# A third buffer for the experts' gate and up weights, a loop body of six experts, and variance tiles of 99 columns

## The reference

```python
def layernorm(x):                       # 34 half-norms in the kernel, two halves of 296 tokens
    m = mean(x); v = mean((x - m) ** 2)
    return (x - m) / sqrt(v + eps)

# experts: each of the 16 takes up to 74 tokens (CAP), I = 1024
h = gelu(x_e @ Wg[e].T) * (x_e @ Wu[e].T)      # gate and up: 256 -> 1024 each
out[tokens of e] += score * (h @ Wd[e].T)      # down: 1024 -> 256, scattered back
```

## Time and profile before

| | us |
|---|---|
| median of three runs | 789.15 |
| the profiled execution, its time | 787.6 |
| its span, first to last instruction | 785.8 |
| PE busy | 757.9 (96%) |
| tokens, block 0 and routing (0 to 131) | 131 |
| experts (131 to 267.7) | 136.7 |
| one encoder layer (380.5 to 451.2) | 70.7 |

### The profile page before, as it was taken

How to read it: one execution, slowest core, us unless ns; L and a number is a source line. 1 busy time by engine, 2 the same in 40 slices (tenths; PEclk the granted TensorE clock), 3 DMA queues, 4 the chain that set the end, 5 groups by cost and what they waited for, 6 DMA issues and landing times.

```text
span 785.8 us, 19872 instructions
## 1 busy us (share of the span) xinstructions
PE 757.9 (96%) x7780; PEld 701.5 (89%) x7780; DVE 555.1 (71%) x1209; ACT 426.7 (54%) x816; POOL 247.6 (32%) x299
## 2 busy tenths in 40 slices
PE   9999999899899899999999999999999999999988
PEld 8898779898898898999899999989899999989758
DVE  6787593344453377787879787787879787776796
ACT  3387422222122265757776786877678677735421
POOL 0002130211111003643462465256346614633020
PEclk9999999899999999999999999999999999999999
DMA  6001745989999220101200310111031003200001
GB/s 199 1 11 45 316 144 185 387 316 378 375 381 380 84 111 2 41 15 54 75 20 13 107 40 13 42 65 40 13 107 40 0 13 107 110 2 1 1 1 32
DMA packets 16726, 83.82 MB, mean 107 GB/s; under 512 B 2848, under 2 KB 8496, under 8 KB 10672
## 3 DMA queue, kind: packets, MB, share of 16 engines
q1 hardware_dynamic: 16688, 83.30, 29.0%
HBM read 80.50 MB, written 2.79 MB: 106 GB/s over the span
## 4 chain that ended last, share of the span: by engine, by line
PE 38%; issue 25%; POOL 19%; DVE 8%; DMA 8%; ACT 3%; POOLq 0%; SPq 0%; DVEq 0%; ACTq 0%
DMA arena<-ew_in 8%; POOL W_L L2058 7%; PE bank L1179 6%; POOL HF_L L2116 4%; POOL arena L2034 3%; PE bank L741 3%; PE bank L1212 3%; POOL WQKV_L L2058 3%; PE bank L765 2%; PE bank L891 2%; PE bank L1068 2%; PE bank L924 2%; PE bank L807 1%; POOL SQ L2077 1%; PE bank L1160 1%
## 5 line engine op out<-in xcount | busy, mean ns | idle before, releaser
L2034 POOL TENSOR_TENSOR arena<-arena,srec 111x456 f32<-111x456 f32 x56 | 52.3, 961 | 122.7 <-DVE srec L2211 122.7
L1179 PE MATMUL bank<-XGS,arena 128*64 128x74 f32 x2048 | 74.5, 231 | 9.6 <-DMA arena<-ew_in 7.1
L1179 PEld LDWEIGHTS bank<-XGS,arena 128*64 128x64 f32 x2048 | 70.5, 139 | 13.7 <-issue 13.4
L2058 POOL TENSOR_TENSOR W_L<-LW,W_H 128x256 fp32r<-128x256 f32 x96 | 68.5, 749 | 36.9 <-DVE XHL L2622 33.5
L2116 POOL TENSOR_TENSOR HF_L<-arena,HF_H 128x296 fp32r<-128x296 f32 x48 | 43.9, 937 | 76.8 <-ACT HF_H L1949 76.8
L807 PE MATMUL bank<-XHL,W_H 128*128 128x296 f32 x288 | 65.1, 307 | 0.0
L1949 ACT ACTIVATE arena<-bank,vec 128x296 f32<-128x296 f32 x96 | 48.8, 509 | 20.4 <-PE bank L807 15.5
L1376 PE MATMUL bank<-HF_L,W_H 128*128 128x296 f32 x192 | 57.4, 299 | 0.0
L1376 PE MATMUL bank<-HF_H,W_H 128*128 128x296 f32 x192 | 57.4, 299 | 0.0
L1376 PE MATMUL bank<-HF_H,W_L 128*128 128x296 f32 x192 | 57.3, 299 | 0.0
L891 PE MATMUL bank<-arena 114*128 114x111 f32 x448 | 55.1, 276 | 0.7 <-issue 0.6
(11 more groups left out here) (282 smaller groups left out, 2052.3 us busy)
## 6 DMA issues: line engine op xcount, KB each, us to landing
arena<-ew_in SPq DMA_DIRECT2D x16, 2048.0 KB, 10.3
arena<-ew_in SPq DMA_DIRECT2D x16, 1024.0 KB, 7.1
LW<-lw_in SPq DMA_DIRECT2D x12, 1024.0 KB, 4.9
LW<-lw_in SPq DMA_DIRECT2D x6, 768.0 KB, 4.4
fp_weights<-arena SPq DMA_DIRECT2D x1, 2048.0 KB, 6.4
arena<-fp_weights SPq DMA_DIRECT2D x1, 2048.0 KB, 7.3
arena<-patches_in SPq DMA_DIRECT2D x2, 864.0 KB, 7.8
LW<-lw_in SPq DMA_DIRECT2D x6, 256.0 KB, 2.6
```

The costliest lines, as they stand in the source:

```text
L1179: last = mm(o[lo:lo + COL_TILE, m * CAP:(m + 1) * CAP], w[:, kc, at:at + COL_TILE], XGS[:, s, kc, :], start=(kc == 0), stop=(kc == C - 1))
L2034: nc.gpsimd.tensor_tensor(v, v, srec[0:QROWS, s:s + 2, :].unsqueeze(3).to_broadcast([QROWS, 2, C * JH, KEYS]), ALU.mult).then_inc(p_ready, 1)
L2058: last = nc.gpsimd.tensor_tensor(low[:, cols], value[:, cols], high[:, cols], ALU.subtract)
```

## The change

*A third buffer.* `GU_THIRD`, 4,096 columns, lies over `R` to `OB`; `XGS` and `EO` move behind it. Gate and up weights now rotate over three places (`GU`), down weights over two as before (`DOWN`), so that the pattern of an expert repeats every six. SP loads gate and up of expert 2 into `GU_THIRD` when the second half of the normalised tokens `U` is written (`u_ready` 2), ahead of the store of positions; and when the up product of expert k - 1 is through, `load_ahead(k)` loads gate and up of k + 2 instead of k + 1. Down of k + 1 and the routes go as before.

*The loop.* PE's body has six steps, n from 1 to 6, and runs twice; steps 13 and 14 are written out behind it. SP's body has six as well.

*The tiles.* `var_tiles` gives three starts, 0, w and nt - w, with w a third of the columns rounded up: 99 of 296, 96 of 288. The products, roots, reciprocals, subtractions and transposes work on w columns or partitions.

```diff
-        XGS = nc.alloc_sbuf_tensor_at("XGS", [P, 2, C, CAP], F32, offset=R_BASE)
+        GU_THIRD = nc.alloc_sbuf_tensor_at("GU_THIRD", [P, EGU_N], F32, offset=R_BASE)
+        XGS_BASE = R_BASE + 4 * EGU_N
+        XGS = nc.alloc_sbuf_tensor_at("XGS", [P, 2, C, CAP], F32, offset=XGS_BASE)
...
+        GU_RING = 3
+        GU = [EW[0][:, 0:EGU_N], EW[1][:, 0:EGU_N], GU_THIRD[:, :]]
...
         def var_tiles(nt):
 
-            return (0, P), (P, P), (nt - P, nt - 2 * P)
+            w = third(nt)
+            return 0, w, nt - w
+
+        def third(nt):
+
+            return -(-nt // 3)
...
+            sp.wait_ge(u_ready, 2)
+            load_gate_up(2, 2)
             sp.wait_ge(pos_cast, 1)
...
-            def load_expert(e, s, route=True):
-
-                sp.wait_ge(u_psum, e * 2 - 2)
-                load_gate_up(e, s)
-                if route:
-                    sp.wait_ge(shot_ready, e - 2)
-                    load_route(e - 1, 1 - s)
-                sp.wait_ge(d_psum, e - 1)
-                load_down(e, s)
-
-            load_expert(2, 0, False)
-            with sp.Fori(1, E // 2 - 1) as i:
-                for s in (1, 2):
-                    load_expert(i * 2 + s, s % 2)
-            load_expert(E - 1, 1)
+            def load_ahead(k, n):
+
+                sp.wait_ge(u_psum, k * 2)
+                load_gate_up(k + 2, (n + 2) % GU_RING)
+                if not isinstance(k, int) or k > 1:
+                    sp.wait_ge(shot_ready, k - 1)
+                    load_route(k, n % 2)
+                sp.wait_ge(d_psum, k)
+                load_down(k + 1, (n + 1) % 2)
+
+            load_ahead(1, 1)
+            with sp.Fori(0, 2) as i:
+                for n in range(2, 8):
+                    load_ahead(i * 6 + n, n)
...
-                        last = mm(ln_bank(seq, h)[:, at:at + VAR_W], sq[:, h, c, t0:t0 + P], ones[:, 0:VAR_W],
+                        last = mm(ln_bank(seq, h)[0:w, at:at + VAR_W], sq[:, h, c, t0:t0 + w], ones[:, 0:VAR_W],
...
-                    last = nc.tensor.transpose(ln_bank(seq, h)[:, t0:t0 + P], ln_rs[:, h, t:t + 1].to_broadcast([P, P]),
-                                               ident)
+                    last = nc.tensor.transpose(ln_bank(seq, h)[:, t0:t0 + w], ln_rs[0:w, h, t:t + 1].to_broadcast([w, P]),
+                                               ident[0:w, 0:w])
...
-            expert_step(0, 0, 1, 1, None)
-            with pe.Fori(1, E // 2) as i:
-                expert_step((i, -1, -1), 1, (i, 0, 0), 0, (i, -1, -2))
-                expert_step((i, 0, 0), 0, (i, 0, 1), 1, (i, -1, -1))
+            expert_step(0, 0)
+            with pe.Fori(0, 2) as i:
+                for n in range(1, 7):
+                    expert_step(i, n)
+            for n in range(E - 3, E - 1):
+                expert_step(0, n)
```

More of the change, by code:

```diff
@@ L300, in build @@
             PB.append(v_.bitcast(BF16)[:, 0:N])
+        GU_RING = 3
+        GU = [EW[0][:, 0:EGU_N], EW[1][:, 0:EGU_N], GU_THIRD[:, :]]
+        DOWN = [EW[s][:, EGU_N:EW_N].rearrange("p (m n) -> p m n", m=EM) for s in range(2)]
+        DOWN_FLAT = [EW[s][:, EGU_N:EW_N] for s in range(2)]
         v_, at = cut(at, C * E * CAP)
@@ L432, in build @@
         ld_qkv, ld_wo, ld_w1, ld_w2, ld_lvec = (sem(n) for n in ("ld_qkv", "ld_wo", "ld_w1", "ld_w2", "ld_lvec"))
-        ld_gu, ld_down, ld_route = ([sem(f"{n}{s}") for s in range(2)] for n in ("ld_gu", "ld_down", "ld_route"))
+        ld_gu = [sem(f"ld_gu{s}") for s in range(GU_RING)]
+        ld_down, ld_route = ([sem(f"{n}{s}") for s in range(2)] for n in ("ld_down", "ld_route"))
         route_stored, out_stored = sem("route_stored"), sem("out_stored")
@@ L761, in ln_var_of @@
                     pe.wait_ge(ln_squared, ln_count(seq, h))
-                for t, (t0, _) in enumerate(var_tiles(nt)):
+                w = third(nt)
+                for t, t0 in enumerate(var_tiles(nt)):
                     for c in range(nch):
                         at = VAR_AT + t * VAR_W
-                        last = mm(ln_bank(seq, h)[:, at:at + VAR_W], sq[:, h, c, t0:t0 + P], ones[:, 0:VAR_W],
+                        last = mm(ln_bank(seq, h)[0:w, at:at + VAR_W], sq[:, h, c, t0:t0 + w], ones[:, 0:VAR_W],
                                   start=(c == 0), stop=(c == nch - 1))
@@ L934, in patch_stats @@
                         constant_products(bank[4], 3)
-                    for t, (t0, _) in enumerate(var_tiles(NP_HALF)):
-                        last = mm(bank[5][:, at + t * VAR_W:at + (t + 1) * VAR_W], R[:, h, k, t0:t0 + P], ones_p[:, 0:VAR_W],
+                    w = third(NP_HALF)
+                    for t, t0 in enumerate(var_tiles(NP_HALF)):
+                        last = mm(bank[5][0:w, at + t * VAR_W:at + (t + 1) * VAR_W], R[:, h, k, t0:t0 + w], ones_p[:, 0:VAR_W],
                                   start=True, stop=True)
@@ L1198, in up_free, with expert_down @@
                 pe.wait_ge(hh_ready, idx(e) * 2)
-            def expert_down(e, s):
-                pe.wait_ge(ld_down[s], group(e) * 16 + 16)
+            def expert_down(e):
+                s = e[1] % 2
+                pe.wait_ge(ld_down[s], (e[0] * 3 + e[1] // 2) * 16 + 16)
                 pe.wait_ge(hh_ready, idx(e) * 2 + 2)
-                if not isinstance(e, int) or e > 0:
+                if e[1] > 0:
                     pe.wait_ge(eot_ready, idx(e))
                     pe.wait_ge(eot_split, idx(e))
-                w = EW[s][:, EGU_N:EW_N].rearrange("p (m n) -> p m n", m=EM)
+                w = DOWN[s]
                 for c in range(C):
@@ L1583, in ln_root @@
                 act.wait_ge(ln_var, ln_count(seq, h))
-                f(ln_sd[:, h, :], LNB[h][:, VAR_AT:VAR_AT + 3 * VAR_W:VAR_W], ACT.Sqrt, bias=eps1[:, :]).then_inc(ln_std, 1)
+                w = third(ln_geometry(seq)[1])
+                f(ln_sd[0:w, h, :], LNB[h][0:w, VAR_AT:VAR_AT + 3 * VAR_W:VAR_W], ACT.Sqrt, bias=eps1[0:w, :]).then_inc(ln_std, 1)
             def exponent(r, p):
@@ L1613, in enc_root @@
                 act.wait_ge(ln_var, ln_count(LN_ENC, h))
-                f(ln_sd[:, h, :], ln_bank(LN_ENC, h)[:, VAR_AT:VAR_AT + 3 * VAR_W:VAR_W], ACT.Sqrt, bias=eps_sq[:, :], scale=1.0 + EPS
+                w = third(NHALF)
+                f(ln_sd[0:w, h, :], ln_bank(LN_ENC, h)[0:w, VAR_AT:VAR_AT + 3 * VAR_W:VAR_W], ACT.Sqrt, bias=eps_sq[0:w, :], scale=1.0 + EPS
                   ).then_inc(ln_std, 1)
@@ L1640, in square_mean @@
                 act.wait_ge(patch_stats_ready, h + 1)
-                f(mean_sq[:, h, :], bank[5][:, MU_AT:MU_AT + 3 * VAR_W:VAR_W], ACT.Square).then_inc(mean_squared, 1)
+                w = third(NP_HALF)
+                f(mean_sq[0:w, h, :], bank[5][0:w, MU_AT:MU_AT + 3 * VAR_W:VAR_W], ACT.Square).then_inc(mean_squared, 1)
             def token_root(h):
@@ L1647, in token_root @@
                 act.wait_ge(ln_var, ln_count(LN_TOK, h))
+                w = third(NP_HALF)
                 for t in range(3):
-                    last = f(ln_sd[:, h, t:t + 1], LNB[h][:, VAR_AT + t * VAR_W:VAR_AT + t * VAR_W + 1], ACT.Sqrt,
-                             bias=eps_var[:, h, t:t + 1])
+                    last = f(ln_sd[0:w, h, t:t + 1], LNB[h][0:w, VAR_AT + t * VAR_W:VAR_AT + t * VAR_W + 1], ACT.Sqrt,
+                             bias=eps_var[0:w, h, t:t + 1])
                 last.then_inc(ln_std, 1)
@@ L2159, in ln_recip @@
                 dve.wait_ge(ln_std, ln_count(seq, h))
-                v.reciprocal(ln_rs[:, h, :], ln_sd[:, h, :]).then_inc(ln_rstd, 1)
+                w = third(ln_geometry(seq)[1])
+                v.reciprocal(ln_rs[0:w, h, :], ln_sd[0:w, h, :]).then_inc(ln_rstd, 1)
             def ln_scale(seq, h, out):
```

62 lines of the change are left out of this document (33 added, 29 removed).

## The result

The changed kernel takes 796.86 us (median of 4 runs, 795.32 to 799.77). The kernel before, run beside it, takes 789.47 us (788.42 to 789.85). The ratio is 1.0091, with a 95% interval from 1.0056 to 1.0127. The profiled execution took 796.79 us with a span of 794.9; before it was 787.6 with 785.8. So the span grew by 9.1 us, where the medians give 7.4: the execution profiled before is 1.9 us faster than the median.

A forecast was written before the change was run, and what follows sets the result against it. It took TensorE to bound the layers, and weight waits and late code to delay it in the expert stage. 787.6 + 18.3 (stage) - 6.5 (tiles) = 799.4 us profiled, 801 us as median; range 772 to 822.

The forecast's parts named there:

- The steps of 9 to 11 us: Sign in the expert stage: one expert's step would take 9 to 11 us instead of 8.06.
- What goes, -12.6: Expert stage: losses taken off, 7.1 us of waits for weights and 5.5 us lost in the old loop's first pass.
- step of 8.06 us: Expert stage: one expert's step from gate to gate, read as undisturbed, with no wait between.
- Code blocks, +26.9: Expert stage: 14 steps fetch 22.4 blocks of PE's code anew, at 1.2 us each.
- The jump, +4: Expert stage: the loop's one jump back finds its target gone; 4 us, between 2.1 and 8.9.
- +18.3: Expert stage in sum: 26.9 for blocks plus 4 for the jump, less 5.5 and 7.1 us.
- The clock: Sign for PE: granted clock under 1.00 in more stretches than one; half its first-pass part counted in the block price.
- The tiles, -6.5: Layer norms with 99-column tiles: 5.3 us less in the layers, 1.2 elsewhere; bounds 0 and -9.7.
- I count 5.3 in full: Layers: 24 norms at 0.22 us less each, 5.3 us, counted whole because PE is the bound there.
- The body is kept: Rival, expert stage: the six-step body stays in instruction memory, only 8 steps are new code; 785.5 us, chance 0.20.
- Fetches stay hidden: Rival, expert stage: code fetches cost PE nothing, only the removed waits count; 770 us, chance 0.17.
- middle price of 0.6 a block: Rival, expert stage: body not kept, each code block costs 0.6 us; 787.5 us, chance 0.08.

The follow-up runs named there:

- Light: The changed kernel with most gate, up and down weights of later experts cut to 256 columns, same PE instructions: 773.16 us, ratio 0.9787 to the kernel before.
- body6: The kernel before (128-column tiles, two gate-up slots) with PE's loop body of six experts alone: 804.79 us, ratio 1.0200.
- Unrolled: The changed kernel with all fourteen expert steps of PE written out, no loop and no jump back: 786.26 us, ratio 0.9960 to the kernel before.
- body2: Control: the kernel before, still two slots and a body of two, with expert helpers written as in the changed kernel: 789.06 us, ratio 0.9988.
- tiles: The kernel before with the 99-column tiles alone, two slots and the body of two kept: 782.32 us, ratio 0.9935.
- body4: The kernel before (128-column tiles, two slots) with a loop body of four experts, three passes: 791.28 us, ratio 1.0043.
- body3: The changed kernel with gate-up weights, down weights and tokens each in three slots and PE's body of three steps, four passes: 773.99 us, ratio 0.9792 to the kernel before.

## Why the prediction was right

It said 801 us and slower, for this reason: the third buffer removes the waits for weights, but the body of six doesn't stay in PE's instruction memory and loses more than that. All of it is borne out. Most of the signs that it named are there: 21 more packets (20 forecast), halts in the middle of 64 products, no wait for `ew_in`. The steps of 9 to 11 us are only half there: in the second pass they take 7.85 to 12.29 us and 15.66 at the jump. The terms are another matter; some were off and partly cancelled, so that it is in part luck how close the sum came.

**What goes, -12.6.** *Light* gives the scale: its stage without the jump's 4.35 us is 125.45, so the stage before held 138.79 - 125.45 = 13.3 us of loss. Each of these stages is that of one profiled execution, and the one before was 1.9 us below the median of its runs. The prediction had 7.1 for listed waits and 5.5 for the first pass of code, 12.6. Two of its readings were off. The step of 8.06 us that it took as undisturbed holds 0.2 us of waiting; the true one is 7.85, and the step of 7.86 from 164.23 on stood in the trace that it read. And the 7.1 us isn't the buffer's to claim under slow code: *body6* lost all but 2.2 of them with two slots. As the price of a block was charged in full beside it, the sum still comes out.

**Code blocks, +26.9.** *Unrolled* has them without a jump: 146.10 - 125.45 = 20.65 us for 14 x 1.6 = 22.4 blocks, **0.92 us a block** instead of 1.2. As that execution is 2.6 us above its median, 0.8 is the estimate for a usual one. What was mis-sized is the guess at how often a block is late and the clock falls. Only six of the blocks of *unrolled* held up PE on this line. The price depends on the run of things: one more or one less late block is up to 2 us, and *unrolled* scatters from 782.36 to 789.60 in ten runs, where the kernel before beside it goes from 787.31 to 791.85 in fifteen.

**The jump, +4.** After against *unrolled*: 153.86 - 146.10 = **7.8 us**, near the upper end of 2.1 to 8.9 that the prediction kept. By the medians it would be some 10, above that end, and the blocks would be that much cheaper. With it, 20.65 + 7.8 - 13.3 = +15.1 us, which closes by construction, where +18.3 stood: -6.3 on the blocks, +3.8 on the jump, -0.7 on what goes.

**The clock.** It was foreseen as more stretches under 1.00. Windows of the trace after; the clock is the third number from the end:

```profile
150.40:157.00 6.60, 6.60 (x75) 6.12 (x76) 3.41 (x7) 0.89 (x2) 0.00 (x0) 0.50 1.00 396
184.50:189.50 5.00, 3.06 (x70) 2.98 (x71) 0.92 (x2) 0.51 (x2) 0.62 (x1) 1.00 0.94 345
201.60:204.80 3.20, 2.57 (x42) 2.57 (x44) 1.64 (x5) 0.21 (x1) 1.07 (x1) 0.50 0.97 407
208.40:211.60 3.20, 3.20 (x57) 3.20 (x56) 0.00 (x0) 0.42 (x1) 0.00 (x0) 0.50 0.03 7
256.20:259.40 3.20, 3.20 (x52) 3.20 (x54) 0.00 (x0) 0.42 (x1) 1.28 (x1) 0.50 0.41 164
```

At least 16.2 us ran at the lower level of 1.2 GHz, each time around the end of a halt of 2.17 to 2.64 us (in these rows from 0.6 us ahead of it to 0.6 behind); after the halt of 1.97 us that ends at 186.44 it stayed at 2.4 GHz (second row). The length of the halt doesn't decide it alone: in *body2* a wait of 1.52 us for weights, up to 233.49, was enough, and the mean clock of the stretch around its end was 0.66:

```profile
233.20:236.00 2.80, 2.51 (x50) 2.52 (x52) 1.93 (x5) 0.42 (x1) 0.38 (x1) 0.66 1.07 448
```

The lower clock is the 6.0 us more that PE is busy in the stage after: 6 of the 15 us come through the clock, the rest as idle time.

**The tiles, -6.5.** The span outside the stage is 6.0 us shorter (6.4 in *tiles*), so the size was right and its place wrong. A layer was to fall by 0.88 us, to 69.8. It takes 70.16 to 70.22, 0.5 less than before. PE's busy time did fall by nearly what was worked out, from 69.53 to 69.59 us a layer to this:

```profile
392.73:462.90 70.17, 68.78 (x526) 65.22 (x525) 57.03 (x126) 51.16 (x90) 33.44 (x42) 1.00 0.14 45
```

What failed is "I count 5.3 in full" because PE is the bound. In half of the norms the next thing was late, as the bounds of the term had allowed. One of them before, PE and then DVE (first the six variances, then eight products as cover, then the turning back, which waits for `ln_rs`):

```profile
412.83 0.86 PE L765 MATMUL bank<-ones_d,SQ 128*128 128x64 f32 x6
413.53 1.09 PE L891 MATMUL bank<-arena 114*128 114x111 f32 x8
414.80 0.54 PE L774 MATMUL bank<-const,ln_rs 128*128 128x128 f32 x3 [0.18 <-DVE ln_rs L2160]
...
412.45 2.21 DVE L2223 TENSOR_SCALAR OB<-bank,lvec 96x148 f32<-96x148 f32 x6
414.59 0.16 DVE L2160 RECIPROCAL ln_rs<-ln_sd 128x3 f32<-128x3 f32 x1
```

And the same norm after:

```profile
424.93 0.72 PE L783 MATMUL bank<-ones_d,SQ 128*99 128x64 f32 x6
425.48 1.10 PE L910 MATMUL bank<-arena 114*128 114x111 f32 x8
426.90 0.47 PE L793 MATMUL bank<-const,ln_rs 99*128 99x99 f32 x3 [0.32 <-DVE ln_rs L2183]
...
424.55 2.21 DVE L2246 TENSOR_SCALAR OB<-bank,lvec 96x148 f32<-96x148 f32 x6
426.68 0.16 DVE L2183 RECIPROCAL ln_rs<-ln_sd 99x3 f32<-99x3 f32 x1
```

The six variances take 0.55 us instead of 0.70 (from their start to the next group's), just the 25 ns each that were forecast. But the reciprocal stands on DVE behind six scalings of `OB` that end at the same distance as before, so PE waits 0.32 us instead of 0.18: the gain of these six products is given back. PE's waits for `ln_rs` in the four layers, before and after:

```profile
PE bank L774 <- DVE ln_rs L2160: 1.4, 8, 0.2
```

```profile
PE bank L793 <- DVE ln_rs L2183: 2.5, 8, 0.3
```

Two norms of a layer's four wait there, and the 1.1 us more are 0.27 a layer. The front, where only a quarter was counted, gave 1.8 us. In *tiles* it gave 2.5 (first gate at 128.48 against 130.96), so that isn't the early load's doing.

**The size that stays.** The runs show that a body of 1,616 matmuls and loads stays and one of 2,424 doesn't. The Trainium skill's page "Runtime: NRT & Kernel Launch", section "Instruction fetch mechanics", gives 2,048 for TensorE, which lies between; no run here is closer to it. Its "mostly hidden" for the crossing of a block is what *light* shows. Under the weight stream it doesn't hold: 11 halts of up to 2.6 us.

**The rivals.** "The body is kept" falls with the 26 packets in the stage, and *body4* and *body3* show from what size on it would have been right. "Fetches stay hidden" (770 us) is right for *light* alone, at 773. The middle price of 0.6 a block was too low, as was the 4 us for the jump under the weights.

## What to carry to other kernels

Before you write out a loop body for the sake of one more buffer, count the engine's instructions between two jumps: a body that stays in instruction memory jumps back for nothing, and one that doesn't is fetched on every pass, and late while the data that it was to wait less for fills the DMA engines. If three buffers are wanted, give every ring the same period, so that the body is as long as the period and no longer: here that turned a loss of 0.9% into a gain of 2.1%. And where a shorter step on the bounding engine feeds a chain, look at what the next engine still has queued ahead of its part.

## What the runs showed of the hardware

Three things I hadn't expected. A jump back to code that is kept costs nothing to be seen (steps of 7.86 to 7.88 us in *body3*, with a jump in them or not), while one to code that is gone costs 4.4 us even with the DMA engines nearly idle (0.19 busy in *light*), and lowers the clock: the 64 products behind it took 3.73 us instead of 2.29. Blocks that are fetched in a straight line are free there: *light* fetched 27 in its stage, with one halt of 0.63 us beside that at the jump. And in *body3* ten steps ran with the DMA engines busy 0.97 and PE without a gap; it was late code, not the bandwidth of the weights, that kept PE waiting in the kernel after.
